# Gated cross-attention and a routed expert layer on one core: VectorE's order in a step, its constants, and the order inside the slots

## The reference, cut to what matters

```
x1 = layernorm(x)                         # per row
k, v = split(ctx @ W_src.T + b_src) * mask;  q = (x1 @ W_tgt.T + b_tgt) * mask
o  = softmax(q k / 4, masked) v           # 8 heads of 16
x  = x + tanh(g_xattn) * (concat(x1, o) @ W_out.T + b_out)
x2 = layernorm(x)
p  = softmax(x2 @ router.T)               # 8 experts; the two best, their weights made to sum to 1
x  = x + tanh(g_ffn) * sum over the two:  weight * (gelu(x2 @ w1[e]) @ w2[e])
```

## Time and profile before

| | |
|---|---|
| time, median of 3 runs (lowest to highest) | 332.65 us (332.07 to 334.12) |
| time of the profiled execution | 334.15 us |
| its span, first to last instruction | 332.3 us |
| PE, DVE, ACT, POOL busy | 296.3, 219.0, 194.0, 220.5 us |
| mean granted TensorE clock | 0.97 of full speed |

### The profile page before, as it was taken

One profiled execution on the slowest core, in us unless ns is written; L12 is line 12 of the kernel. 1 busy time (PEld: TensorE's weight loads), 2 busy tenths in 40 slices (PEclk: granted clock), 3 DMA queues, 4 the chain that ended last, 5 costly groups with the idle time before them and its releaser, 6 DMA issues.

```text
span 332.3 us, 10883 instructions
## 1 busy us (share of the span) xinstructions
PE 296.3 (89%) x3521; PEld 266.6 (80%) x3521; DVE 219.0 (66%) x909; ACT 194.0 (58%) x502; POOL 220.5 (66%) x301
## 2 busy tenths in 40 slices
PE   8789999999998999896888979999998999999920
PEld 3668788787876878785668969999998999999920
DVE  2776567689899998889568796435853433434653
ACT  3466869888795877856575427547444444444300
POOL 3735455354787888888455878778877876555860
PEclk9997999999999999999799997999999999999995
DMA  6643522202151211850134222311352432229346
GB/s 215 183 120 126 186 71 70 63 22 92 52 128 34 68 50 49 248 146 26 54 98 112 66 67 72 91 50 57 98 128 82 137 108 78 68 72 352 102 134 189
DMA packets 41237, 34.60 MB, mean 104 GB/s; under 512 B 5045, under 2 KB 36951, under 8 KB 41185
## 3 DMA queue, kind: packets, MB, share of 16 engines
q1 hardware_dynamic: 32608, 23.10, 24.8%
q0 software_dynamic: 4320, 8.47, 7.2%
q10 hardware_dynamic: 4256, 2.36, 2.4%
HBM read 22.35 MB, written 12.01 MB: 103 GB/s over the span
## 4 chain that ended last, share of the span: by engine, by line
PE 44%; POOL 22%; issue 16%; DVE 8%; ACT 5%; DMA 3%; POOLq 0%; SPq 0%; ACTq 0%; DVEq 0%
POOL rows L653 10%; PE ps_sc L1596 9%; POOL picked L671 8%; PE ps_proj L1609 4%; PE ps_o L1609 4%; PE ps_o L1555 3%; PE ps_proj L1490 3%; PE ps_proj L1493 3%; PE ps_sc L1439 3%; PE ps_sc L1434 2%; PE ps_proj L1501 2%; PE ps_o L1475 2%; ACT xr L801 2%; DVE rowmax L1225 2%; PE ps_proj L1502 2%
## 5 line engine op out<-in xcount | busy, mean ns | idle before, releaser
L671 POOL DMA_INDIRECT picked<-yo,xg x71 | 71.6, 1008 | 16.3 <-issue 11.6
L1596 PE MATMUL ps_sc<-xt,w1c 128*128 128x128 f32 x568 | 76.2, 278 | 3.2 <-issue 2.4
L653 POOL DMA_INDIRECT rows<-xr,posi x64 | 63.1, 985 | 18.0 <-issue 18.0
L1596 PEld LDWEIGHTS ps_sc<-xt,w1c 128*128 128x128 f32 x568 | 69.8, 193 | 4.2 <-issue 4.1
L835 ACT ACTIVATE probT<-ps_sc 128x512 f32<-128x512 f32 x71 | 42.4, 598 | 43.5 <-PE ps_sc L1596 42.6
L724 ACT ACTIVATE probT<-ps_sc,pencol 128x512 f32<-128x512 f32 x64 | 43.6, 683 | 23.4 <-PE ps_sc L1453 13.1
L1225 DVE TENSOR_REDUCE rowmax<-ps_sc 128x4 f32<-128x512 f32 x64 | 43.7, 685 | 15.5 <-PE ps_sc L1453 13.2
L591 POOL TENSOR_TENSOR kblkr<-kT,headcol 128x256 fp32r<-128x256 f32 x32 | 19.7, 616 | 39.1 <-ACT kT L761 38.8
L1609 PE MATMUL ps_proj<-w2s,probT 128*128 x288 | 38.9, 279 | 0.0
L1609 PE MATMUL ps_o<-w2s,probT 128*128 x280 | 37.1, 275 | 0.0
L1345 DVE COPY w1c<-w1s 128x512 f32 x71 | 31.6, 449 | 7.0 <-PE ps_sc L1596 2.3
(11 more groups left out here) (169 smaller groups left out, 618.0 us busy)
## 6 DMA issues: line engine op xcount, KB each, us to landing
xg<-rows SPq DMA_DIRECT2D x71, 65.0 KB, 1.8
ctxs<-ctxT SPq DMA_DIRECT2D x32, 128.0 KB, 2.4
xs<-x SPq DMA_DIRECT2D x8, 256.0 KB, 3.0
maskbc<-mask SPq DMA_DIRECT2D x8, 256.0 KB, 4.7
w1s<-w SPq DMA_DIRECT2D x4, 512.0 KB, 3.8
w2s<-w SPq DMA_DIRECT2D x8, 256.0 KB, 4.8
maskbc<-picked SPq DMA_DIRECT2D x4, 512.0 KB, 6.5
out<-xs ACTq DMA_DIRECT2D x6, 256.0 KB, 2.3
```

The costliest lines, as they stand in the source:

```text
L653: nc.gpsimd.indirect_dma_start(out=rows, out_offset=bass.IndirectOffsetOnAxis(ap=posi[:, i, pick, b:b + 1], axis=0), in_=xr[:, i, pick, b, ...
L671: nc.gpsimd.indirect_dma_start(out=picked, out_offset=bass.IndirectOffsetOnAxis(ap=xg[:, r, D + 1:D + 2].bitcast(I32), axis=0), in_=yo[:, ...
L1596: last = nc.tensor.matmul(ps_score[j % DEEP][:, c * 128:(c + 1) * 128], w1c[:, j % DEEP, c * 128:(c + 1) * 128], xt[:, j % XRING, :], star ...
```

## The change

DVE's `label` and `position` move behind the queries and the residual. The late constants are made in three blocks, at steps (1, 1), (2, 1) and (2, 3). In a slot DVE's copy to `w1c` comes first, ahead of the pieces. The two long sums of `carry` become a piece of their own, and the middle plan's eight pieces stand in slots 6 to 11, 13 and 14. POOL's factors of group 7 move from step (10, 2) into slot 9, ahead of the sends of that slot. ACT normalises group 7 one sequence at a time in slots 14 to 17, at the end of the slot.

```diff
+AHEAD = (10, 2)
+MIDDLE_AT = (6, 7, 8, 9, 10, 11, 13, 14)
...
 # POOL, step
-                if k == 2 and G is not None:
-                    pool.wait_ge(s_ln2, G + 1)
...
+                if k == 2 and G is not None and (g, k) != AHEAD:
+                    factors(G)
 # POOL, slot, between the scatter and the sends
+                if n == slot_at(*AHEAD) - 3:
+                    factors(AHEAD[0] - LAG_OUT)
 # ACT, step
-                if k == 3 and G is not None:
-                    box, used = outbox(G)
...
+                if k == 3 and G is not None and g != AHEAD[0]:
+                    normalise_again(G, range(GROUP))
 # ACT, slot, after gelu
+                b = n - slot_at(*AHEAD) - 2
+                if 0 <= b < GROUP:
+                    normalise_again(AHEAD[0] - LAG_OUT, (b,))
 # DVE, constants
-            def late_setup():
+            def late_zeros():
                 nc.vector.memset(padrow[:, 0:D], 0.0).then_inc(s_pad0, 1)
...
+            def late_rows():
                 dve.wait_ge(s_tables, 16)
...
+            def late_jumps():
                 nc.vector.memset(jump[:, :], 1.0).then_inc(s_late, 1)
...
 # DVE, middle plan
+                def sum_open():
+                    sums(last, stop, 2, late_exp, late_row)
                 def carry():
                     count = stop - last
-                    sums(last, stop, 2, late_exp, late_row)
...
 # DVE, step
-                G = group(g, LAG_SEND)
-                if k == 0 and G is not None and not in_slots(G):
-                    label(G)
-                    position(G)
                 G = group(g, 0)
                 if k == 1 and G is not None:
                     moments(G, s_st1, st1, mv1, ve1, nm1, (s_nm1, s_ln1))
...
                     nc.vector.tensor_tensor(x1, ps_proj[:, 3 * T:4 * T], x1, ALU.add).then_inc(s_xo, 1)
+                G = group(g, LAG_SEND)
+                if k == 0 and G is not None and not in_slots(G):
+                    label(G)
+                    position(G)
...
-                if (g, k) == (1, 3):
-                    late_setup()
+                if (g, k) == (1, 1):
+                    late_zeros()
+                if (g, k) == (2, 1):
+                    late_rows()
+                if (g, k) == (2, 3):
+                    late_jumps()
 # DVE, slot: the copy to w1c moves from behind the pieces to here
             def slot(n):
+                j = slot_of(n, 0)
+                if j is not None:
+                    if j % REGS == 0:
+                        turn["experts"] = experts_of(mybir.EngineType.DVE, j, min(REGS, SLOTS - j))
+                    wait(dve, f_up, j - DEEP + 1)
+                    nc.vector.tensor_copy(
+                        w1c[:, j % DEEP, :],
+                        w1s[:, turn["experts"][j % REGS], :].rearrange("p o h -> p (o h)")).then_inc(f_w1, 1)
...
-                    late_pieces.update(enumerate(middle_plan(), n))
+                    late_pieces.update(zip(MIDDLE_AT, middle_plan()))
```

More of the change, by code:

```diff
@@ L641, in step, with factors @@
                         ALU.add).then_inc(s_xb, 1)
+            def factors(G):
+                pool.wait_ge(s_ln2, G + 1)
+                wait(pool, s_x2n, GROUP * G)
+                nc.gpsimd.tensor_tensor(rs2[:, :], ve2[:, :], minus_half[:, :],
+                                        ALU.pow).then_inc(s_rs2, 1)
+                pool.wait_ge(s_rs2, G + 1)
+                pool.wait_ge(s_nm2, G + 1)
+                nc.gpsimd.tensor_tensor(mr2[:, :], nm2[:, :], rs2[:, :], ALU.mult).then_inc(s_mr2, 1)
             def scatter(G, sends):
@@ L714, in expert_exponents, with normalise_again @@
                                          ACT.Exp).then_inc(s_lexp, 1)
+            def normalise_again(G, seqs_of):
+                box, used = outbox(G)
+                act.wait_ge(s_mr2, G + 1)
+                act.wait_ge(s_x2, G + 1)
+                wait(act, s_send[box], SEND * used)
+                for b in seqs_of:
+                    nc.scalar.activation(
+                        xr[:, box, 0, b, 0:D], xs[:, bass.ds(GROUP * G + b, 1), :].rearrange("p o d -> p (o d)"),
+                        ACT.Identity, bias=mr2[:, b:b + 1], scale=rs2[:, b:b + 1]).then_inc(s_x2n, 1)
             def normalise(G, seqs_of):
@@ L1189, in carry @@
                     assert planned[0] == CARRIED
-                return count_full, end_full, pass_ends, write, end_open, pass_open, carry
+                return count_full, end_full, pass_ends, write, end_open, pass_open, sum_open, carry
             def last_plan():
@@ L1339, in slot @@
                     late_pieces[n]()
[L1340 to L1347, removed]
                 j = slot_of(n, LAG_DOWN)
```

## The result

The changed kernel takes 336.51 us (median of 7 runs, 336.05 to 339.73) against 333.79 us (7 runs, 332.07 to 334.12): a ratio of 1.0122, 95% interval 1.0095 to 1.0149. The profiled execution took 336.35 us, its span is 334.5 us against 332.3 before. The forecast was 334.5 us; the result lies in its range, but in the case "slower by over 1%", which had 0.28 against 0.45 for no change.

What follows compares the result with a forecast made beforehand. POOL's fixed list was taken to set slot 41 and PE the rest. Constants -2.4, queries first +2.6 and clock behind slot 41 +1.7 gave +1.9 us, 334.5 us on the median of 332.65; range 328.0 to 338.0 us.

Steps and rivals of the forecast that it cites:

- slower by over 1%: Outcome for the whole kernel: slower by more than 3.3 us; chance 0.28.
- no change: Outcome for the whole kernel: within about 1%, 3.3 us, of the time before; chance 0.45.
- The bound: Slot 41's start is set by POOL's fixed list of 72.6 us from 178.28; after slot 41 PE alone counts.
- Constants: Early attention steps: PE's 1.58 us stand and the half clock after it go; 2.4 us gained, ends 0.3 and 3.1.
- Queries and residual first: Steps (5, 0) to (8, 0): moved `label` and `position` meet POOL's instructions and delay FAR; 2.6 us lost.
- a share of further holds: Steps (5, 0) to (8, 0): if one more DVE instruction is held by POOL, each loses 0.6 us more.
- my upper end: Steps (5, 0) to (8, 0): 3.8 us lost if `label` is held too; 1.4 us without it.
- Slots: PE reaches slot 41 3.3 us sooner, stands 4.3 us at POOL's unchanged list, then loses 1.7 us to half clock.
- let DVE through: Rival, attention: `label` and `position` slip between POOL's instructions and the clock holds at slot 41; -4.8 us, 327.9 us; chance 0.26.
- further stretch at half clock: Rival, attention: PE's stands at the maxima's transpose make two groups run cold; 3.2 us more, 337.7 us; chance 0.14.
- the factors did not stop POOL: Rival, slot 9: early factors make POOL stand 1.1 us waiting for `ve`, delaying the end equally; 335.6 us; chance 0.10.
- The sum: Whole kernel: -2.4 + 2.6 + 1.7 = +1.9 us on the 332.65 us median, 334.5 us.

Runs made afterwards that it cites:

- e6: Changed kernel with the last group's eight scatters all issued in slot 29 of POOL's list; 330.57 us, ratio 0.9915 to the kernel before.
- e12: Kernel before with the last group's eight scatters in slot 29 as its only edit; 331.60 us, ratio 0.9936.
- e2: Kernel before with only queries and residual put ahead of `label` and `position`; 336.03 us, ratio 1.0073.
- e3: Kernel before with the slots' edits alone (weights first, sums split, factors sooner, normalisations spread); 336.65 us, ratio 1.0090.
- e4: Changed kernel with POOL's residual add put ahead of the two scatters of its step; 333.67 us, ratio 1.0003 to the kernel before.
- e10: Changed kernel with residual add first and last scatters in slot 29, but the `w1c` copy back behind the plan's piece; 326.92 us.
- e11: Changed kernel with residual add first and last scatters in slot 29, but factors and normalisations back in their old places; 330.93 us.
- e1: Kernel before with the constants made in three blocks as its only edit; 331.49 us, ratio 0.9957.
- e9: Changed kernel with residual add first and last scatters in slot 29, without any of the slots' edits; 329.86 us.

## Why the prediction was right, and where it was not

- **The bound** was read rightly: POOL's list sets slot 41 and PE the rest. What PE won ahead of it was stood away. That slot 41 begins at the same hundredth is chance: by the forecast the 0.99 us won ahead of slot 0 should have moved it, and a list that is 0.96 us longer ate them. Moving the last scatter took the stand away (e6) and was worth little while PE was late (e12).
- **Constants**, -2.4 us: 2.86 us in the profiled execution. FAR of (2, 0) starts at 20.64 us (22.46 before) and the stand is gone. But 1.1 us of it is a stretch at 0.59 that the kernel before does not have in every execution. Three experiments leave the constants as they were: in e2 and e12 PE stands the same 1.58 us, and the clock stays full; in e3 it stands 1.57 us, and from 26 to 30 us the clock is 0.57. The stretch in e12, columns as above:

```profile
26.00:30.00 4.00, 3.61 (x67) 2.97 (x64) 3.84 (x19) 2.82 (x8) 2.37 (x5) 1.00 0.19 60
```

  That part was charged as certain from one execution. About 1.8 us is what does not hang on that stretch: 2.86 less the 1.09 us by which e12 is earlier at step (2, 2).
- **Queries and residual first**, +2.6 us: 1.85 us, from PE's transposes of `oT` (2.86 us earlier than before at step (5, 1), 1.01 us at (9, 2)). At (5, 0) to (8, 0) it lost 0.5, 0, 0.8 and 0.6 us, where I had 0, -0.4, 0.8 and 0.9 and a share of further holds. This is the step that failed in its reason. I let `placed` be held by POOL's residual add; but in (6, 0) to (8, 0) the residual itself waits for the end of this add, by a semaphore that stands in the code (`s_xb`) and cost nothing as long as `label` and `position` stood ahead of it. I had listed who waits for DVE's moved instructions, and not for whom the instructions moved ahead wait. At (5, 0), which I took at nothing because POOL has sent nothing yet, holds alone cost the 0.5 us, and e4 leaves them. The Trainium skill ("SBUF — State Buffer", Who interferes with whom) says that DVE's copies in a two-port mode and its products of two SBUF tensors share a port pair with GpSimd, and that the later one waits. That they hold each other the trace shows: the copy of `label`, 0.17 us alone, takes 0.37 until POOL's key product ends, and in e4 `tw` takes 1.42 us beside the add. Which of the two waits stays open: `tw` is recorded 0.12 us ahead of the add (113.86 and 113.98) and still ends with it. In (7, 0) DVE has already waited for the add when it comes to `label`, so that only the shorter key products and `pen` hold it, by 0.2, 0.3 and 0.2 us for the copy of `label`, `placed` and `posi`. The loss came to 1.85 us, not to the 3.8 us of my upper end.
- **Slots**: PE's gain 2.9 for 3.3 us, the stand 4.85 for 4.3, the stretch behind it 2.03 for 1.7. Against it the list was said to be unchanged and became 0.96 us longer. The issues of the same 26 scatters took 25.7 instead of 25.2 us and the 17 small instructions between them 4.5 instead of 4.2; e3 shows that it comes with the slots' edits, and what delays them stays open. I named the copy to `w1c` as what PE stood for; e10 and e11 show that factors and normalisations decide, and that the copy first is worth at most 0.5 to 0.7 us behind them.
- **The rivals**: POOL did not let DVE through, in the changed kernel; no further stretch at half clock came in the attention, where PE's stands at the transpose reached 1.4 us; the factors did not stop POOL.
- **The sum** was right because its errors cancel: 0.5 us too little gain and 0.75 us too much loss ahead of slot 0, against 1.0 us of list and 0.5 us behind slot 41 that it lacked. It gave +1.9, the span has +2.2 and the medians +2.7. Another 1.1 us of the distance from 334.5 to 336.51 is the base: the median of the three runs shown was 332.65, that of seven is 333.79.

Left open: why PE's time from (9, 0) to (9, 2), 11.3 to 13.2 us, differs among executions of nearly the same program.

## What to carry to other kernels

Before an instruction is moved ahead of others, list the semaphores on which it waits: a wait that costs nothing behind other work becomes the path when that work goes behind it. If an engine's fixed list sets a later point, shorten what stands in the list ahead of the point: what the other engines win while the list runs is stood away, and here the stand of 4.85 us cost PE another 2.0 us of clock behind it. An edit that is a loss alone may be a gain once that list is shortened: here the slots' edits cost 0.9% and then gained 1.1%.

## What was not expected of the hardware

PE's stand of 2.44 us was followed by four microseconds at a clock of 0.57 to 0.64 in all five traces that have it (before, e1, e2, e9, e12), and stands of 4.6 to 4.85 us by six at 0.54 to 0.67 in the changed kernel, e3 and e4. The stand of 1.58 us was followed by 0.59 before and 0.57 in e3, and by full clock in e2 and e12, so one execution does not tell what a stand of this length costs. Half clock need not be lost time: the slots' edits took the 2.44 us and the stretch behind them away and gained 2.9 us in the slots, where PE then waited for other engines instead (busy 2.95 of the 4 us from 200). That leaves at most 0.5 us for the stretch, if the whole stand was won; no run has the one without the other.
